# Quarter-wise tail, prefetched first-choice weights, and per-step sums in a one-core hybrid block

## What is computed

```python
def _mamba3(...):                       # run forward and backward; both results are added
    ...
    yg = y.reshape(b, l, D_INNER) * jax.nn.silu(z)
    yn = yg * jax.lax.rsqrt(jnp.mean(yg * yg, -1, keepdims=True) + EPS) * norm_w
    return yn @ out_proj
...
def step(h, p):                         # routed layer, scanned over 33 blocks
    op = jnp.argmax(h[0, 0, :NOPS])     # 19 choices, from the first token
    ...                                 # attention with the weights of op
    h = jnp.where(p['am'][op], y, h)
    z = jax.nn.relu(h @ p['w1'][op] + p['b1'][op]) @ p['w2'][op] + p['b2'][op]
    h = jnp.where(p['fm'][op], z, h)
...
t = t + _L3_attn_ref(_ln_t(t), ...)
t = t + _L3_ffn_ref(_ln_t(t), ...)
```

## Time and profile before

| | us |
|---|---|
| median of 3 runs (lowest, highest) | 711.55 (710.62, 718.04) |
| profiled execution | 713.98 |
| its span, first to last instruction | 712.2 |

### The profile page before, as it was taken

How to read it: one execution, slowest core, us unless ns; L and a number is a source line. 1 busy time by engine, 2 the same in 40 slices (tenths; PEclk the granted TensorE clock), 3 DMA queues, 4 the chain that set the end, 5 groups by cost and what they waited for, 6 DMA issues and landing times.

```text
span 712.2 us, 10651 instructions
## 1 busy us (share of the span) xinstructions
PE 497.7 (70%) x3952; PEld 276.9 (39%) x3953; DVE 315.8 (44%) x723; ACT 331.1 (46%) x1101; POOL 0.2 (0%) x4
## 2 busy tenths in 40 slices
PE   5654555556986599999656666666648999898634
PEld 2221222223653477667323333333314554464111
DVE  1174000107864778888550000000077995588223
ACT  2232333332764667777523333333435565865311
POOL 0000000000000000000000000000000000000000
PEclk9555555556899899999965555555589999999876
DMA  4000000000000000000000000000040000000000
GB/s 181 0 2 1 0 1 1 0 1 0 2 1 1 0 2 2 1 1 1 1 0 1 1 0 1 1 0 1 0 118 1 2 2 1 1 2 1 0 13 30
DMA packets 4417, 6.71 MB, mean 9 GB/s; under 512 B 650, under 2 KB 4106, under 8 KB 4236
## 3 DMA queue, kind: packets, MB, share of 16 engines
q1 hardware_dynamic: 4364, 6.01, 2.8%
HBM read 3.38 MB, written 0.52 MB: 5 GB/s over the span
## 4 chain that ended last, share of the span: by engine, by line
PE 57%; DVE 16%; ACT 16%; issue 7%; SPq 2%; DMA 1%; DVEq 1%
PE ps L295 16%; ACT arena L313 10%; PE ps L273 4%; PE ps L278 3%; PE ps L753 3%; PE ps L731 3%; PE ps L588 2%; PE ps L719 2%; PE ps L575 2%; PE ps L235 2%; PE ps L571 2%; PE ps L715 2%; PE ps L602 2%; DVE arena L1159 2%; DVE arena L1168 2%
## 5 line engine op out<-in xcount | busy, mean ns | idle before, releaser
L295 PE MATMUL ps<-arena,wsb 16*16 16x16 f32 (+1 forms) x1024 | 131.4, 206 | 116.6 <-ACT arena L313 111.1
L313 ACT ACTIVATE arena<-ps 16x16 f32<-16x16 f32 (+1 forms) x512 | 96.0, 188 | 191.8 <-PE ps L295 191.8
L295 PEld LDWEIGHTS ps<-arena,wsb 16*16 16x16 f32 (+1 forms) x1024 | 76.5, 118 | 199.9 <-ACT arena L313 186.5
L319 DVE TENSOR_TENSOR X<-X,ps 128x128 f32<-128x128 f32 x16 | 4.6, 288 | 199.7 <-PE ps L278 199.7
L1286 DVE TENSOR_TENSOR arena<-arena,ps 128x512 f32<-128x512 f32 x96 | 62.2, 683 | 16.4 <-PE ps L731 8.0
L901 ACT ACTIVATE arena<-ps,arena 128x128 f32<-128x128 f32 (+1 forms) x128 | 52.4, 418 | 31.0 <-DVE arena L1160 30.9
L981 ACT ACTIVATE arena<-ps 128x512 f32<-128x512 f32 x96 | 53.9, 595 | 25.0 <-PE ps L719 17.2
L1159 DVE TENSOR_REDUCE arena<-ps 128x2 f32<-128x512 f32 (+1 forms) x48 | 33.0, 688 | 18.5 <-PE ps L571 11.1
L588 PE MATMUL ps<-wsb,arena 128*128 128x128 f32 x192 | 30.4, 281 | 13.7 <-DVE arena L1168 13.7
L575 PE MATMUL ps<-arena 128*128 128x256 f32 x128 | 34.6, 393 | 0.0
L1168 DVE TENSOR_TENSOR arena<-arena 128x512 f32<-128x512 f32 x48 | 33.2, 692 | 1.7
(11 more groups left out here) (232 smaller groups left out, 731.5 us busy)
## 6 DMA issues: line engine op xcount, KB each, us to landing
arena<-xn SPq DMA_DIRECT2D x16, 128.0 KB, 2.7
wsb<-weights SPq DMA_DIRECT2D x1, 1916.5 KB, 9.6
wsb<-weights SPq DMA_DIRECT2D x1, 549.5 KB, 4.6
X<-x SPq DMA_DIRECT2D x1, 512.0 KB, 3.5
out<-X SPq DMA_DIRECT2D x2, 256.0 KB, 2.3
csb<-consts SPq DMA_DIRECT2D x1, 160.0 KB, 9.6
arena<-w SPq DMA_DIRECT2D x2, 64.0 KB
arena<-w_biases SPq DMA_DIRECT2D x2, 17.0 KB
```

What stands on the lines that cost most here:

```text
L295: nc.tensor.matmul(step_columns(k, rows, r), w_state, states[0:rows, :, :, t].rearrange("p g j -> p (g j)"), start=False, stop=True, skip_ ...
L313: nc.scalar.activation(states[0:rows, :, :, t + 1].rearrange("p g j -> p (g j)"), step_columns(t // STEP_BANK, rows, t % STEP_BANK), func) ...
```

## The change

Six edits, all at or for the end of the program.

1. The backward end goes by quarters. `project_last(j)` makes mean square and output of one quarter (256 columns) in banks of its own; `sigma_last(j)` and `add_last(j)` follow on ACT and DVE. Quarter 0 is put inside the pipeline: on PE ahead of the last pair of units, on ACT ahead of the last square, on DVE ahead of the last gate.
2. The layer norm that follows goes by halves: centre, sum of half 0, then of half 1, on PE; square, Ln, Exp per half on ACT.
3. `pick(0)` runs after `normalise(0)`, ahead of `normalise(1)`.
4. SP fetches the weights of the first block for all 19 choices into `first_experts` (in the place of `states`), after its 16 restacking DMAs. The first step runs as a copy of the step code ahead of the loops and copies from there.
5. The sum `X + xn` is formed at the end of each step (and once before the first) into a buffer `total`, and SP stores `total`.
6. The table holds row offsets ((block + 1) * 19) instead of block numbers; `look` and `step` add where they multiplied and added.

```diff
+            sp.wait_ge(s["candidates ready"], 1)
+            at = sp.alloc_register("candidate")
+            for o in range(NOPS):
+                sp.reg_load(at, candidates[0:1, o:o + 1])
+                flat = nc.s_assert_within(sp.snap(at) + (o - NOPS), 0, NB * NOPS - 1)
+                sp.dma_start(first_experts[:, o, 0:HID], by_flat(w1)[bass.ds(flat, 1), :, :]
+                             .to_broadcast([G, C, HID])).then_inc(s["first experts"], 16)
+                sp.dma_start(first_experts[:, o, HID:], by_flat(w2_biases)[bass.ds(flat, 1), :, :]
+                             .rearrange("a c d -> (a c) d")).then_inc(s["first experts"], 16)
+            sp.wait_ge(s["normalised"], 9)
...
+            def project_last(j):
+                pe.wait_ge(s["M squares"], J + j + 1)
...
+                for bank, lhs, rhs, done in ((LAST_MEAN[j], W("avg_e"), zf, s["M mean squares last"]),
+                                             (LAST_OUT[j], wout[:, 1, :], yg, s["M out last"])):
+                    for gp in range(2):
+                        mm = nc.tensor.matmul(ps[2 * C * gp:2 * C * (gp + 1), bank, 0:T], lhs,
+                                              rhs[:, j, gp * T:(gp + 1) * T], start=True, stop=True)
...
+                if d == 1:
+                    act.wait_ge(s["M forward added"], 1)
+                    sigma_last(0)
                 squares(d, J - 1)
...
-            def feed_forward(i, op, n, step, look):
-                dve.wait_ge(s["R weights"], n * 32 + 32)
-                nc.vector.tensor_copy(expert, arriving).then_inc(s["R weights taken"], 1)
+            def feed_forward(flat, n, step, fetched, source, look):
+                if source is None:
+                    dve.wait_ge(s["R weights"], fetched * 32 + 32)
+                    nc.vector.tensor_copy(expert, arriving).then_inc(s["R weights taken"], 1)
+                else:
+                    dve.wait_ge(s["first experts"], 32 * NOPS)
+                    nc.vector.tensor_copy(expert, first_experts[:, bass.ds(source, 1), :].rearrange("p a w -> p (a w)"))\
+                        .then_inc(s["R weights taken"], 1)
...
             dve.sem_inc(s["R weights taken"], 1)
+            normalise(0)
+            dve.wait_ge(s["normalised"], 9)
             pick(0)
-            routed("vector", dve, attention, feed_forward, pick)
-            for h in range(2):
-                nc.vector.tensor_tensor(halves(X)[h], halves(X)[h], halves(xn)[h], ALU.add).then_inc(s["X final"], 1)
+            normalise(1)
+            dve.wait_ge(s["normalised"], 10)
+
+            def add_up():
+                for h in range(2):
+                    nc.vector.tensor_tensor(halves(total)[h], halves(X)[h], halves(xn)[h], ALU.add).then_inc(s["R sum"], 1)
+
+            add_up()
+            routed("vector", dve, attention, feed_forward, pick, add_up)
```

In `routed` itself:

```diff
-                entry = nc.s_assert_within(eng.snap(at) * NOPS + NOPS + eng.snap(op), 0, (NB + 1) * NOPS - 1)
+                entry = nc.s_assert_within(eng.snap(at) + eng.snap(op), 0, (NB + 1) * NOPS - 1)
...
+                    add_up()
...
+            with eng.If_lt(at, limit):
+                step(initial=True)
             outer, middle, inner = STEPS
-            with eng.Fori(0, outer), eng.If_lt(at, NB), eng.Fori(0, middle), eng.If_lt(at, NB), eng.Fori(0, inner), eng.If_lt(at, NB):
+            with eng.Fori(0, outer), eng.If_lt(at, limit), eng.Fori(0, middle), eng.If_lt(at, limit), eng.Fori(0, inner), eng.If_lt(at, limit):
                 step()
```

More of the change, by code:

```diff
@@ L457, in _, with feed_forward @@
-            routed("sync", sp, attention, feed_forward)
+            def feed_forward(flat, n, step, fetched, source):
+                if source is not None:
+                    sp.sem_inc(s["sync read the first pick"], 1)
+                if source is None:
+                    sp.wait_ge(s["R weights taken"], n + 1)
+                    sp.dma_start(arriving[:, 0:HID], by_flat(w1)[bass.ds(flat, 1), :, :]
+                                 .to_broadcast([G, C, HID])).then_inc(s["R weights"], 16)
+                    sp.dma_start(arriving[:, HID:], by_flat(w2_biases)[bass.ds(flat, 1), :, :]
+                                 .rearrange("a c d -> (a c) d")).then_inc(s["R weights"], 16)
@@ L458, in _ @@
+            steps = routed("sync", sp, attention, feed_forward)
+            sp.wait_ge(s["first experts"], 32 * NOPS)
             for h in range(2):
-                sp.wait_ge(s["X final"], h + 1)
-                sp.dma_start(out.rearrange("(j g) c h w -> (g c) j (h w)", g=G)[:, 2 * h:2 * h + 2, :], Xj[:, 2 * h:2 * h + 2, :])\
-                    .then_inc(s["stored"], 16)
+                sp.wait_ge(s["R sum"], sp.snap(steps) * 2 + (h + 1))
+                sp.dma_start(out.rearrange("(j g) c h w -> (g c) j (h w)", g=G)[:, 2 * h:2 * h + 2, :],
+                             total.rearrange("p (j t) -> p j t", j=J)[:, 2 * h:2 * h + 2, :]).then_inc(s["stored"], 16)
@@ L819, in attention, with feed_forward @@
                 pe.wait_ge(s["R attention written"], n + 1)
-            def feed_forward(i, op, n, step):
+            def feed_forward(flat, n, step, fetched, source):
                 pe.wait_ge(s["R weights taken"], n + 2)
@@ L944, in sigmas, with sigma_last @@
                     nc.scalar.activation(halves(oat)[h], halves(oat)[h], ACT.Exp, scale=-0.5).then_inc(s["M sigma"], 1)
+            def sigma_last(j):
+                cols = oat[:, j * T:(j + 1) * T]
+                act.wait_ge(s["M mean squares last"], j + 1)
+                nc.scalar.activation(cols, ps[:, LAST_MEAN[j], 0:T], ACT.Ln, bias=W("eps")).then_inc(s["M log last"], 1)
+                act.wait_ge(s["M log last"], j + 1)
+                nc.scalar.activation(cols, cols, ACT.Exp, scale=-0.5).then_inc(s["M sigma last"], 1)
             def squares(d, j):
@@ L989, in _, with attention @@
                     act.preload_act_table(ACT.Silu)
-            act.wait_ge(s["M forward added"], 1)
-            sigmas(1)
-            norm_scalar(act, 4)
-            def attention(i, op, n):
+            for j in range(1, J):
+                sigma_last(j)
+            for h in range(2):
+                act.wait_ge(s["centred"], 8 + h + 1)
+                nc.scalar.activation(halves(sq)[h], ps[:, h, :], ACT.Square, scale=C ** -0.5).then_inc(s["squares"], 1)
+                act.wait_ge(s["variance"], 8 + h + 1)
+                nc.scalar.activation(halves(sq)[h], ps[:, 6 + h, :], ACT.Ln, bias=W("eps")).then_inc(s["log variance"], 1)
+                act.wait_ge(s["log variance"], 8 + h + 1)
+                nc.scalar.activation(halves(sq)[h], halves(sq)[h], ACT.Exp, scale=-0.5).then_inc(s["1/sigma"], 1)
+            def attention(flat, n):
                 for m, dst in enumerate((rq[:, 0, :], rq[:, 1, :], oat[:])):
@@ L1250, in _, with add_last @@
             ins.then_inc(s["M decay operands"], 1)
+            def add_last(j):
+                cols = slice(j * T, (j + 1) * T)
+                dve.wait_ge(s["M sigma last"], j + 1)
+                dve.wait_ge(s["M out last"], j + 1)
+                link(nc.vector.tensor_tensor(oat[:, cols], oat[:, cols], ps[:, LAST_OUT[j], 0:T], ALU.mult))
+                ins = nc.vector.tensor_tensor(X[:, cols], X[:, cols], oat[:, cols], ALU.add)
+                if j % 2 == 1:
+                    ins.then_inc(s["X halves"], 1)
             for d, name in enumerate(("fwd", "bwd")):
@@ L1376, in feed_forward @@
                 dve.sem_inc(s["vector pick step"], 1)
+                if source is not None:
+                    dve.wait_ge(s["sync read the first pick"], 1)
                 nc.vector.max_index(op_at[:], best[:], ps[0:1, 7, P:P + NOPS]).then_inc(s["op picked"], 1)
```

80 lines of the change are left out of this document (49 added, 31 removed).

## The result

| | before | after |
|---|---|---|
| median, us (lowest to highest) | 711.53 (710.62 to 718.04) | 703.73 (703.11 to 704.57) |
| profiled execution, us | 713.98 | 704.57 |
| its span, us | 712.2 | 702.8 |

The ratio is 0.9876, with a 95% interval of 0.9837 to 0.9915; by the medians the kernel is 7.8 us faster, 1.1%. The forecast was 701.7 (698 to 705.5), faster by over 1%. Single executions in a slower state (three of those counted further down, 720.0 to 1358 us) are left out of every median.

A forecast was written before the change was run, and what follows sets the result against it. It took a chain of dependent work, 57% PE, not one full engine, as the bound. From median 711.55, -8.3 - 0.2 + 1.2 - 2.7 + 0.1 = -9.9 us gave 701.7 us, range 698 to 705.5.

The forecast's parts named there:

- Part 1: Backward end by quarters: last gate 1.2 us later, all of `X` ready 2.3 us earlier, half 0 4.2 us earlier.
- Part 2: Layer norm by halves, pick after half 0: pick at 669.7, norm done at 672.2, midway between the clock bounds.
- Part 3: First step's weights at hand: no DMA on the path, copy at 675.3 against 683.57, minus 8.3 us.
- Part 4: The steps: offsets save 0.2 us; PE's jump over unloaded attention code before step 2 adds 1.2 us (0 to 2.5).
- Part 5: Way out of the loops: the end waits for a sequencer instead of the store, minus 2.7 us.
- Part 6: Hidden work: SP's 38 DMAs end near 575, 100 us early; one extra DVE operation adds 0.1 us.
- no late PE: Rival: PE not late in step 2, blocks fetched ahead or faster; 700.5 us, 699 with the higher clock; chance 0.27.
- The reading binds: Rival: before the first step PE or ACT needs more blocks, or DVE's reading is dearer; 705.0 to 707; chance 0.11.
- Refills held up: Rival: weights fetched ahead delay PE's instruction blocks in 528 to 575; plus 8.7 us, 710.4; chance 0.03.
- SP isn't done: Rival: SP's fetches unfinished when DVE wants the first weights; slower, 745 us at 10 us a choice; chance 0.04.

The follow-up runs named there:

- third group: Follow-up runs e9 to e12, made on one chip beside the kernel before, which ran at 713.0 us; the only group holding the changed kernel itself.
- e7: Changed kernel with the backward output projection, sigmas and adds by halves behind the last square, as before; 708.34 us, ratio 0.9925.
- e5: Changed kernel without the fetch ahead: SP fetches the first choice's weights after the pick; 707.15 us, ratio 0.9922.
- e6: Changed kernel with the first pick behind both halves of the norm; 707.8 us, ratio 0.9934.
- e4: Changed kernel with the last gate ahead of the add of quarter 0 on DVE; 703.25 us, ratio 0.9835.
- e10: The changed kernel again, unchanged; 705.85 us, ratio 0.9911.
- e3: Changed kernel with loops of 6, 4, 3 instead of 4, 3, 3, so ten failing checks instead of seven; 706.93 us, ratio 0.9875.
- e8: Changed kernel with the sum of `X` and `xn` formed once, behind DVE's loops; 708.43 us, ratio 0.9901.
- e12: Same kernel as e5 (changed kernel without the fetch ahead), run in another group; 705.76 us, ratio 0.9909.
- e1: Changed kernel with one looped copy of the step's code on PE and ACT; DVE and SP keep the separate first step; 700.48 us, ratio 0.978.
- e2: Changed kernel with the attention code, never run on these inputs, left out on all four engines; 704.12 us, ratio 0.9834.
- e9: Changed kernel with e1's single copy, gate ahead of quarter 0, quarter 0 behind the last pair, earlier PE look, one check fewer; 701.9 us, ratio 0.9853.
- e11: e9 with one copy of the step on all engines and no fetching ahead; 702.39 us, ratio 0.9854.

## Why the prediction came out right, step by step

The time and the direction held, but by terms that were off both ways, and in part by luck. The tail fell by 8.3 us, not 10.0; the profiled span came within 0.5 us of the 702.3 forecast because that execution also reached the tail 1.1 us earlier, which no term of the forecast says. In the third group the same kernel ran at 705.85, just above the range, beside a kernel before that was slower as well (713.0); there the gain was 0.9% by the ratio. So "faster" is safe and "by over 1%" is not.

**Part 1 held.** The gate starts 1.95 us behind the last product, against 0.8 before: 1.15 us later, forecast 1.2. Half 0 of `X` was forecast at 662.8 on a scale on which the last product ends at 656.73, so 6.1 us behind it, and half 1 at 8.0; measured 5.8 and 7.4. e7 gives the gain: 2.9 us at the copy.

**Part 2: mechanism right, clock better than taken.** I took the middle between 1.2 and 2.4 GHz. The windows of the changed kernel (columns as in the earlier trace rows):

```profile
668.00:669.00 1.00, 0.00 (x0) 0.00 (x0) 0.08 (x1) 0.86 (x2) 0.00 (x0) 1.00 0.00 0
671.00:672.00 1.00, 0.00 (x0) 0.00 (x0) 0.00 (x0) 0.00 (x0) 0.00 (x0) 0.50 0.09 25
```

The clock stayed at 2.4 GHz through the norm, up to 670, where before it read 0.50 in 668 to 669: the centring of a half took 1.14 us for two records, against 3.31 for four. It also stayed there through the projections, where before it read 0.50 from 661 to 664. e7, with projections by halves and the norm as changed, falls in the projections and not in the norm. So the norm's gain in clock goes with the norm by halves, in which PE pauses between its operations (idle 0.69 us before L808, where before it ran from 667.05 to 672.44 without a gap), and not with the earlier start that the quarters give. That the pauses are the reason is likely, but no run tests it. It was at 1.2 GHz by 671, after PE had had nothing to do from the last sum of squares (667.5) on. On the old scale the pick ends at 668.7 and the norm at 670.7, one and one and a half us ahead of the values taken, just below the lower bounds of the forecast (668.9 and 670.8).

**Part 3: the size right, the reason wrong, and that was luck.** The copy was forecast 8.3 us earlier and came 8.7 earlier. That is a sum of two errors, since the norm ended 1.5 us earlier than taken and DVE's reading was 4.2 us (669.61 to 673.84), not 3.1: its register load (0.80) is as dear as SP's, and the jump over its own attention code was left out. The claim "no DMA is on the path any more" was true and worth next to nothing. What I compared it with was the old order, in which the pick came last. The right comparison is with all other edits in place (e5): 18.52 against 18.18. The forecast also said that PE would be ready 4.5 us after the pick; e6 shows 7.0, and e4, where PE binds too, 7.15 (666.03 to 673.18). The 4.5 us end where the packet ends. In e6 the packet starts 3.5 us behind the pick and takes 1.2, and 2.3 more pass before the product. "Just hidden behind DVE" held but for 0.2 us (0.6 in e10), and only because DVE's reading was under-priced too.

**Part 4: the right stall, at two fifths of its size.** A q8 packet ahead of step 2, and PE rather than DVE late there, both came. The DMA queues of the changed kernel in 685 to 686:

```profile
q8 instruction: 1, 0.02, 9.5%
```

The packet takes 1.52 us (9.5% of 16 engines for 1 us), from 685.08 to 686.6, and the forecast had 1.65 for a block. But PE's first product is at 688.52. Between the packet's end and that product lie 1.9 us that I did not have; in 686 to 688 no instruction packet moves. That is the failed step: "needs 3 us for `look` and the branches, and then 1.65 us for the block". It put the whole wait at a packet. The first part of it was right: from the end of PE's work of step 1 (681.98) to the packet it takes 3.1 us. The other profiles in which PE has two copies of the code show the same three pieces, and only the packet varies:

| us | end of PE's step 1 to packet | packet | packet's end to PE's first product |
|---|---|---|---|
| changed kernel | 3.1 | 1.5 | 1.9 |
| e3_steps643 | 3.0 | 0.9 | 2.0 |
| e6_latepick | 3.0 | 1.2 | 1.9 |
| e10_again | 3.1 | 1.5 | 1.9 |

(e4, e5, e7, e8 and e12: 3.0 to 3.2, 0.9 to 1.5, 1.8 to 2.0.) The row of e3 comes from its DMA queues in 684 to 685, where the packet starts at 684.2 and PE's first product at 687.05:

```profile
q8 instruction: 1, 0.02, 5.6%
```

So the length of the packet is most of why step 2 differs between these kernels (11.30 in e3, 11.96 in the changed one). Little of the 1.9 us can be PE's ordinary work: in e1 PE goes from the end of step 1 to its first product of step 2, over the same code but without a packet, in 3.5 us (684.11 to 687.59) and waits for DVE's copy in that time. What does fill the 1.9 us the profile doesn't show; it stays open.

Step 2 cost 2.9 us more, not 1.2, beyond the upper end of 2.5. Step 1 was 0.45 us longer, not 0.2 shorter. In this pair it is the clock: 16 records of L881 took 3.80 us, those of L831 3.34, since the clock rose to 2.4 GHz some 6.5 us behind the copy, and 4.5 before the change. But the changed kernel's own two profiles differ by as much.

The Trainium skill, "Runtime: NRT & Kernel Launch", section "Instruction fetch mechanics", has a taken branch to code outside the loaded window wait for its fetch. e1 and e2 agree: with the code at hand or the jump gone, the 3.1 us vanish. Of a window of two pages e1 says the contrary, as the kernel before did: looping back over what the forecast estimated at 58 KB, PE fetched nothing. The same section also gives PE a larger instruction store than other engines, 128 KiB, and with that the trace agrees.

**Part 5 held.** -3.05 us against -2.7. The end waits for a sequencer, PE's (1.3 us), where the forecast summed DVE's and put PE's about as late; e3 puts a failing check at 0.6 us (forecast 0.69), and e8 shows what sums behind the loops would cost, 3.7 us.

**Part 6 held,** as far as it shows. SP is through with its 38 DMAs at 570 and waits 96.6 us for the norm (its waits in the changed kernel):

```profile
SPq L381 <- DVE xn L1395: 96.6, 1, 96.6
```

The 0.1 us for the extra operation in the first recurrence is too small to be seen: profiles of one kernel reach the tail 2.3 us apart.

**The sum.** Against the forecast -10.0 for the tail: copy -0.36, step 1 +0.65, step 2 +1.74, way out -0.35, together +1.7, hence -8.3. The median moved by 7.8. Of the rivals, "no late PE" fell, and e1 shows what it would take: no second copy of the code. "The reading binds" came in part, since DVE's reading was 1.1 us dearer, but the clock of part 2 gave that back. "Refills held up" and "SP isn't done" did not come.

## What to carry to other kernels

Price each edit with the other edits in place, not against the kernel before: an early pick had already taken nearly all of the DMA off the path, and the fetch ahead of it bought 0.2 to 0.3 us at the copy. Code that is never run still costs where it is jumped over for the first time (3 us here for PE's attention code, of which the transfer itself is about half), so duplicating a loop's body to save a wait on one engine can make another wait; keep one copy on the engine with the most instructions. When a store seems to bind the end, look at who else must finish: here work moved ahead of the loops' way out gained 3 us, and then a sequencer's failing checks at 0.6 us each set the end.

## What the runs showed of the hardware beyond expectation

- From the pick to PE's first product, across one jump over attention code, it takes 7.0 us (e6), with an instruction packet of 1.2 us on that way. A later jump into code not yet loaded costs 3.1 us (changed kernel), with a packet of 1.5. Such a packet takes 0.9 to 1.5 us in the nine profiles with two copies on PE, and 1.8 to 2.0 us pass between its end and the first product of step 2 in each.
- A backward branch across the same code costs no packet and no wait (e1, e9, e11).
- PE's clock stayed at 2.4 GHz through a norm by halves, in which PE pauses between its operations (changed kernel and e7), and fell to 1.2 in the norm before, in which PE ran 5.4 us without a gap. Why it falls isn't shown.
- The same kernel reaches the same instruction at times 2.3 us apart in two executions (655.66 and 653.35 for the last product), so parts of a kernel are better compared from a common event than from the span's start.
